# Level 64 of a triangular inverse: half of the chunks multiplied in the other order, tiles in pairs, in a fused layer stack

## The reference

```python
mixed = jax.nn.silu(_causal_conv(hidden_states @ w_qkv, conv_w))
q, k, v = jnp.split(mixed, [KEY_DIM, 2 * KEY_DIM], axis=-1)
...
def step(state, xs):
    q_t, k_t, v_t, g_t, b_t = xs
    state = state * jnp.exp(g_t)[..., None, None]
    kv = jnp.einsum('bhk,bhkv->bhv', k_t, state)
    delta = (v_t - kv) * b_t[..., None]
    state = state + jnp.einsum('bhk,bhv->bhkv', k_t, delta)
    out = jnp.einsum('bhk,bhkv->bhv', q_t, state)
    return (state, out)
...
o = o * jax.nn.silu(z.astype(jnp.float32))
o = o * jax.lax.rsqrt(jnp.mean(o * o, axis=-1, keepdims=True) + EPS)
return (o * norm_gamma).reshape(Bq, Sq, VALUE_DIM) @ w_out
```

## Time and profile before

| | |
|---|---|
| median of three runs | 1398.15 us (1395.53 to 1399.49) |
| the profiled execution | 1400.72 us, span 1398.9 us |
| PE busy | 1289.0 us (92%) |
| DVE, ACT, POOL busy | 969.0, 790.9, 753.2 us |
| mean granted clock | 0.961 |
| DMA | 171.71 MB, 123 GB/s |

### The profile page before, as it was taken

One profiled execution on the slowest core, in us unless ns is written; L12 is line 12 of the kernel. 1 busy time (PEld: TensorE's weight loads), 2 busy tenths in 40 slices (PEclk: granted clock), 3 DMA queues, 4 the chain that ended last, 5 costly groups with the idle time before them and its releaser, 6 DMA issues. The chain is left out here.

```text
span 1398.9 us, 24967 instructions
## 1 busy us (share of the span) xinstructions
PE 1289.0 (92%) x8680; PEld 875.8 (63%) x8680; DVE 969.0 (69%) x1922; ACT 790.9 (57%) x1947; POOL 753.2 (54%) x1245
## 2 busy tenths in 40 slices
...
GB/s 87 113 74 118 101 146 142 98 183 118 109 170 110 153 134 97 180 114 125 166 111 154 133 95 179 116 201 68 0 1 304 275 1 1 68 72 94 125 187 186
DMA packets 233180, 171.71 MB, mean 123 GB/s; under 512 B 163746, under 2 KB 202998, under 8 KB 230240
## 3 DMA queue, kind: packets, MB, share of 16 engines
...
## 5 line engine op out<-in xcount | busy, mean ns | idle before, releaser
L723 PE MATMUL psum_banks<-main_hT,gdn_w_in 128*128 128x512 f32 x512 | 255.2, 609 | 7.4 <-DMA gdn_w_in<-in_w_in 4.1
L1227 DVE SCALAR_TENSOR_TENSOR heads_y<-psum_banks,gdn_conv_w,heads_y 128x1021 f32<-128x1021 f32 (+2 forms) x192 | 244.7, 1275 | 21.7 <-ACT heads_y L1033 17.5
L1522 POOL TENSOR_TENSOR heads_XT<-heads_XT,heads_tmp 128x126 f32<-128x126 f32 (+22 forms) x496 | 198.6, 400 | 38.9
L1519 POOL TENSOR_TENSOR heads_tmp<-heads_XT,heads_A 128x126 f32<-128x126 f32 (+22 forms) x496 | 189.6, 382 | 41.5 <-PE psum_banks L902 1.8
L723 PEld LDWEIGHTS psum_banks<-main_hT,gdn_w_in 128*128 128x128 f32 x512 | 93.5, 194 | 62.1 <-issue 52.7
L849 PE MATMUL psum_banks<-heads_w_z,main_hT 128*128 128x256 f32 x512 | 128.8, 384 | 0.0
L871 PE MATMUL psum_banks<-heads_ogT,heads_w_o 128*128 128x512 f32 x240 | 126.4, 609 | 0.2 <-issue 0.2
L849 PEld LDWEIGHTS psum_banks<-heads_w_z,main_hT 128*128 128x128 f32 x512 | 95.2, 191 | 25.2 <-issue 14.4
L1033 ACT ACTIVATE heads_y<-psum_banks,gdn_conv_w 128x1024 f32<-128x1024 f32 x64 | 71.3, 1114 | 69.3 <-PE psum_banks L723 69.0
L1057 ACT ACTIVATE heads_O<-psum_banks,heads_coef 128x128 f32<-128x128 f32 x224 | 69.6, 363 | 70.5 <-PE psum_banks L756 70.3
L1490 POOL TENSOR_TENSOR heads_og<-heads_og,heads_fac 128x512 f32<-128x512 f32 x60 | 61.2, 1041 | 80.1 <-DVE heads_fac L1294 80.1
...
...
## 6 DMA issues: line engine op xcount, KB each, us to landing
...
heads_ogT<-outputs_by_features SPq DMA_DIRECT2D x30, 512.0 KB, 3.8
...
gdn_w_in<-in_w_in SPq DMA_DIRECT2D x16, 512.0 KB, 4.3
...
```

What stands on the lines that cost most here:

```text
L723: ins = pe.matmul(out[:, half * 512:(half + 1) * 512], w_in[:, kd_, j * P:(j + 1) * P], hT[:, kd_, half * 512:(half + 1) * 512], start=kd_ ...
L1227: dve.scalar_tensor_tensor(y[j][:, shift:T], src[:, 0:T - shift], conv_w[:, head, j, t:t + 1], y[j][:, shift:T], ALU.mult, ALU.add).then_i ...
L1519: pool.tensor_tensor(tmp[:, 0:n, 0:m], bc_last(XT[:, 0:n, j], m), bc_mid(A0[:, j, j + 1:BLK], n), ALU.mult).then_inc(solve_step.sem, 1)
L1522: pool.tensor_tensor(XT[:, 0:n, j + 1:BLK], XT[:, 0:n, j + 1:BLK], tmp[:, 0:n, 0:m], ALU.add).then_inc(solve_step.sem, 1)
```

## The change

Level 64 takes the chunks in two halves. Chunks 0 to 3 (`y7a`, `u7a`) are computed as before. For chunks 4 to 7 (`y7b`, `u7b`) the product of three is taken in the other order: first the coupling with the second inverse (rows 64 to 127, written to partitions 0 to 63), then the first inverse with that (rows 0 to 63, written to partitions 0 to 63). The intermediate of the second half is copied by ACT into the first rows of `kneg`. On PE the two halves are issued in turn, in two groups instead of three: `y7a` issues both y halves, `u7a` both u halves; `y7b` and `u7b` name only the second bank.

```diff
-                elif name == "y7_0":
-                    for j in range(4):
-                        ins = last_y7(b, j, j, par)
-                    ins.then_inc(full[b].sem, 1)
-                elif name == "y7_1":
-                    b0 = bank_of(h, "u7_0")
-                    for j in range(4):
-                        iy = last_y7(b, j, 4 + j, par)
-                        for i in (2 * j, 2 * j + 1):
-                            iu = last_u7(b0, 0, i, par)
-                    iy.then_inc(full[b].sem, 1)
-                    iu.then_inc(full[b0].sem, 1)
-                elif name == "u7_1":
-                    for i in range(8):
-                        ins = last_u7(b, 1, i, par)
-                    ins.then_inc(full[b].sem, 1)
+                elif name == "y7a":
+                    ba, bb = bank_of(h, "y7a"), bank_of(h, "y7b")
+                    half = C // 2
+                    for j in range(half):
+                        c, d = j, half + j
+                        ia = pe.matmul(bank[ba][64:128, j], kneg[par][0:64, c, 64:128], Xh[0:64, c:IT:C], start=True, stop=True)
+                        ib = pe.matmul(bank[bb][0:64, j], kneg[par][64:128, d, 0:64], Uf[par][64:128, d:IT:C, 64:128], start=True, stop=True)
...
+                elif name == "u7a":
+                    ba, bb = bank_of(h, "u7a"), bank_of(h, "u7b")
+                    right = flat(kneg[par][0:64, 0:4])
+                    for i in range(IT // 2):
+                        e, j = i // 4, i % 4
+                        at, mine = slice(i * 64, (i + 1) * 64), j * HD + e
+                        ia = pe.matmul(flat(bank[ba][:])[0:64, at], Y7[64:128, mine], Uf[par][64:128, e * C + j, 64:128], start=True, stop=True)
+                        ib = pe.matmul(flat(bank[bb][:])[0:64, at], Xh[0:64, e * C + 4 + j], right[:, mine * 64:(mine + 1) * 64],
+                                       start=True, stop=True)
...
```

All rows of the five tables are written anew around it (the last passes take theirs from the same tables). Two lines of them:

```diff
-su5 out0/2:0 ks6 out0/2:1 y7_0/1 p6/-1:0 p6/-1:1 qs6 tx6 out1/1:0 o6 p7/-1:0 su6 p7/-1:1 y7_1/0 u7_0/3 out1/1:1 ks7
+o5 su5 out0/2:0 p6/-1:0 p6/-1:1 ks6 out0/2:1 qs6 tx6 p7/-1:0 out1/2:0 o6 p7/-1:1 out1/2:1 y7a/1 y7b/0 su6 out2/3:0
```

More of the change, by code:

```diff
@@ L202 @@
 PE_PLAN = """
-z0/2:0 tx0 z0/2:1 o0 p0/-1:0 p0/-1:1 su0 p1/-1:0 p1/-1:1 ks1 z1/1:0 qs1 z1/1:1 tx1 norm_q/2 z2/3:0 z2/3:1 o1 su1
-p2/-1:0 p2/-1:1 decay0/1 decay1/2 decay2/3 decay3/0 ks2 qs2 p3/-1:0 tx2 kk0/1 o2 su2 p3/-1:1 ks3 kk1/2 qs3 tx3 attn1/3
-o3 su3 z3/0:0 z3/0:1 p4/-1:0 p4/-1:1 ks4 qs4 p5/-1:0 tx4 p5/-1:1 o4 su4 y6a/1 y6b/2 ks5 attn0/0 qs5 tx5 u6a/1 u6b/2 o5
-su5 out0/2:0 ks6 out0/2:1 y7_0/1 p6/-1:0 p6/-1:1 qs6 tx6 out1/1:0 o6 p7/-1:0 su6 p7/-1:1 y7_1/0 u7_0/3 out1/1:1 ks7
-qs7 out2/2:0 tx7 out2/2:1 o7 out3/3:0 u7_1/0 out3/3:1
+z0/1:0 tx0 z0/1:1 p0/-1:0 p0/-1:1 o0 su0 p1/-1:0 p1/-1:1 ks1 qs1 norm_q/0 z2/2:0 tx1 z2/2:1 o1 su1 z1/3:0 z1/3:1 ks2
@@ L208 @@
+qs2 p2/-1:0 tx2 decay0/3 decay1/2 decay2/1 decay3/0 p2/-1:1 o2 su2 p3/-1:0 p3/-1:1 ks3 kk0/2 qs3 tx3 kk1/3 o3 su3
+z3/2:0 z3/2:1 p4/-1:0 p4/-1:1 ks4 qs4 p5/-1:0 tx4 p5/-1:1 o4 su4 y6a/2 y6b/0 attn0/3 ks5 qs5 u6a/1 u6b/2 tx5 attn1/0
+o5 su5 out0/2:0 p6/-1:0 p6/-1:1 ks6 out0/2:1 qs6 tx6 p7/-1:0 out1/2:0 o6 p7/-1:1 out1/2:1 y7a/1 y7b/0 su6 out2/3:0
+out2/3:1 ks7 qs7 u7a/0 u7b/1 out3/2:0 tx7 out3/2:1 o7
 """
 PE_FIRST = """
-p0/-1:0 p0/-1:1 p1/-1:0 norm_q/2 p1/-1:1 p2/-1:0 decay0/0 decay1/1 decay2/3 decay3/2 p2/-1:1 p3/-1:0 attn1/1 p3/-1:1
@@ L212 @@
-p4/-1:0 kk0/2 p4/-1:1 p5/-1:0 p5/-1:1 p6/-1:0 kk1/2 p6/-1:1 p7/-1:0 attn0/2 p7/-1:1 y6a/3 y6b/2 u6a/3 u6b/0 y7_0/2
-y7_1/2 u7_0/3 u7_1/0
+p0/-1:0 p0/-1:1 p1/-1:0 p1/-1:1 norm_q/2 p2/-1:0 p2/-1:1 p3/-1:0 p3/-1:1 p4/-1:0 decay0/0 decay1/1 decay2/2 decay3/3
+p4/-1:1 p5/-1:0 kk0/0 attn0/0 kk1/2 p5/-1:1 p6/-1:0 p6/-1:1 p7/-1:0 y6a/2 y6b/3 p7/-1:1 u6a/3 u6b/0 attn1/1 y7a/0
+y7b/2 u7a/3 u7b/0
 """
 PE_SECOND = """
-p0/-1:0 z0/1:0 p0/-1:1 out0/2:0 tx0 p1/-1:0 z0/1:1 o0 su0 p1/-1:1 ks1 qs1 norm_q/0 z1/1:0 tx1 z2/3:0 z1/1:1 out2/1:0
@@ L218 @@
-o1 su1 z2/3:1 p2/-1:0 decay0/2 decay1/0 decay2/3 decay3/1 out2/1:1 ks2 qs2 out3/2:0 tx2 p2/-1:1 p3/-1:0 o2 su2 kk0/0
-out0/2:1 p3/-1:1 ks3 qs3 kk1/3 tx3 o3 su3 attn0/3 ks4 p4/-1:0 p4/-1:1 qs4 p5/-1:0 tx4 z3/3:0 p5/-1:1 o4 su4 y6a/2
-y6b/1 ks5 z3/3:1 qs5 tx5 attn1/0 u6a/1 u6b/2 o5 out1/0:0 su5 p6/-1:0 ks6 p6/-1:1 qs6 tx6 p7/-1:0 y7_0/2 out1/0:1 o6
-p7/-1:1 su6 y7_1/2 u7_0/0 out3/2:1 ks7 qs7 tx7 u7_1/1 o7
+z0/2:0 z0/2:1 p0/-1:0 p0/-1:1 tx0 p1/-1:0 o0 z2/1:0 su0 p1/-1:1 ks1 norm_q/0 z2/1:1 z1/2:0 qs1 tx1 z1/2:1 o1 su1
```

81 lines of the change are left out of this document (44 added, 37 removed).

## The result

| | before | after |
|---|---|---|
| median | 1398.82 us (4 runs) | 1420.2 us (4 runs, 1416.67 to 1422.9) |
| the profiled execution | 1400.72 us | 1422.9 us |
| its span, mean granted clock | 1398.9 us, 0.961 | 1421.1 us, 0.954 |

What follows compares the result with a forecast made beforehand. PE, busy 92% of 1398.9 us, was taken to bound the kernel. Level 64 −17.8, pass 0 −2.3, recurrence turns spaced wider −2.6, late transfers +6.5, pass 16 +1.2: −15.0, from 1398.15 to 1383 us, range 1373 to 1392.

Steps and rivals of the forecast that it cites:

- Level 64: PE's y and u groups: 1.20 and 1.27 us instead of 3.74 a pass, saving 17.8 us over 14 passes.
- The late transfers: Waits for late keys, outputs and DVE/ACT results: 0.5 us a pass, 6.5 over 13; bounds 0 and 1.6.
- `su0`: State product at the pass's edge, waiting for keys loaded behind w_o: 0.2 us on average, bounds 0 and 0.8.
- `out2`: Output product waiting for the load of turned outputs, stored later behind two taps: 0.2 us, bounds 0 and 0.5.
- Pass 0, forecast −2.3: Level 64 in pass 0: one round trip between PE and ACT fewer, u group ending at 92.0; −2.3 us.
- I take pass 1 as near: Passes 2 to 14 taken as equal to the profiled whole pass of 56.10 us, pass 1 as near it.
- The base of the new rows: PE's row in an ordinary pass, items summed from start to start: 55.8 us before, 54.5 now.
- Pass 16, forecast +1.2: Recurrence's chain in pass 16: output halves of 0.86 us each between tx6 and su6, su6 and ks7; +1.2 us.
- Pass 15, forecast 0: Recurrence's chain in pass 15 loses and gains about as much: 0, bounds −1.3 and +1.
- slower: the key loads behind w_o: Rival at the pass's edge: PE waits 2.0 us at su0, 0.5 at out2, giving 1411 us; chance 0.05.

Runs made afterwards that it cites:

- the old rows: Kernel before with the new level 64, all five tables of rows as they were but for names; 1419.31 us, ratio 1.0165.
- the queue's row: Changed kernel with SP's row alone reordered: keys' load right behind their store, w_z and gate rows behind the second outputs' load; 1397.92 us, ratio 1.0009.
- where the queue is mended: Changed kernel with the queue's row, here also with q_square ahead of base0 in ACT's first row: 1393.02 us, against 1397.92 without that exchange.

## Why the prediction was wrong

The distance of 37 us to the forecast lies, by the table of the passes, in passes 2 to 14 (14.5), pass 0 (11.8), pass 1 (5.0), pass 15 (3.6) and pass 16 (2.5).

- **Level 64** was right: 1.21 + 1.28 us against 1.20 + 1.27, and the u group's pairs overlap although both write partitions 0 to 63. By the Trainium skill's page "TensorE: Matmul & The Clock Gate", section "Wait — 56ns, not 53.3ns?", which has 62 ns for each matmul where the sequencer decodes in software, the two groups would take an estimated 3.6 us. This case does not agree: the records of a pair start 0.01 us apart and the pairs of the u group 0.055. What I did not see is that a pair needs both banks at once: in the old rows that cost 2.0 us a pass and the clock.
- **The late transfers, forecast +0.5 a pass,** were mis-sized, the largest error. In passes 2 to 14 everything above the base of 54.76 comes to 1.54 a pass, close under the upper bound of 1.6, and the queue's row alone is worth 0.96 of it (56.30 against 55.34). `su0` was the right place: 7.1 us in 12 waits, 0.55 a pass, against 0.2 taken. I sized it with landings measured at a quiet time of the queue: from the first key load's issue to the last landing it is 4.9 us on average at the pass's edge in the kernel after, against 4.3 in the kernel before. `out2`, forecast 0.2, did not wait. `out0`'s load was not in the sum at all; it was waited for three times, 1.4 us each.
- **Pass 0, forecast −2.3, was +9.5.** The step that failed is the one that costed only the round trip of level 64 there. The new first rows of PE, ACT and DVE were never walked. With the three old rows the median is 9.8 us lower; with one entry of ACT's row moved, `q_square` ahead of `base0`, it is 11.7 lower (1420.2 to 1408.5), but 4.9 lower where the queue is mended. The row opens the waits; how much pass 0 loses by them, 100.4 to 108.5 us to the first `tx0`, went with where the clock fell behind them.
- **The 2.3 us themselves** were too many. In the six profiles with pass 0's old rows and the new level, the time from ACT's first copy of level 32's corners (L1129 before) to its last of level 64's is 7.8 us against 8.6 before, and to `inverse0` on DVE 7.9 against 9.2: 0.8 and 1.3 shorter. The y group now waits for all three copies of level 32's corners and starts 2.0 us behind the first instead of 0.6, which the step did not count. And the first `tx0` gained nothing of it: it comes at 97.6 to 100.5, 98.9 on average, against 99.0.
- **"I take pass 1 as near" an ordinary pass** failed too: its row was not walked either. 54.8 us against 51.1; with the old rows of pass 1 and the new level it is 50.9. Of the 3.9 between the last and the first, 2.4 is the row (53.3 in four runs) and 1.5 comes where the clock falls at the pass's start (mean clock 0.97 in it).
- **The base of the new rows**, 54.5 by the sum of the items, is 54.76: right within 0.3. The range missed because the terms against it were taken near their lower ends in the 13 passes, and the rows of passes 0 and 1 at nothing.
- **Pass 16, forecast +1.2, was +3.7**; with the queue's row it is 4.4 shorter, 0.7 under the kernel before. The step had only the output halves between `tx6` and `ks7` and forgot that the keys come late in that pass too, where nothing else covers them. **Pass 15, forecast 0, was +3.6**; what sets its time stays open.
- The rival "slower: the key loads behind w_o", 1411 us at a chance of 0.05, had the sign and one of the mechanisms, but not its size: it had `su0` wait 2.0 us, and the longest such wait in passes 2 to 14 is 0.8. By the runs the queue's row is 17 us (12.5 + 4.4), of which the forecast had some 5 in its 6.5 for what comes late; the rest of the 37 is mostly the rows of passes 0 and 1 and what the clock does there.
